# Gated cross-attention kernel: evictions, column-sum copy and GpSimd normalisation in another order, projection moved forward

## What is computed

```python
x = x + tanh(g_xattn[0]) * L0_xattn(layernorm(x), ctx, ctx, ...)   # pruned attention
x = x + tanh(g_ffn[0])   * L0_ffn(layernorm(x), ...)               # FP4 weights, gated
x = x + tanh(g_xattn[1]) * L1_xattn(ctx, layernorm(x), ...)        # linear attention
x = x + tanh(g_ffn[1])   * L1_ffn(layernorm(x), ...)               # int8 linear

# L0_xattn, one head
scores  = softmax(q @ k.T / 4)
col_sum = scores.sum(over queries)
keep the 460 keys of 512 with the largest col_sum, zero the others
out     = (scores * mask) @ v
```

## Time and profile before

| | us |
|---|---|
| median of 3 runs | 1252.24 |
| lowest and highest | 1250.3, 1255.97 |
| the profiled execution | 1255.39 |
| its span, first to last instruction | 1253.7 |

### The profile page before, as it was taken

One profiled execution on the slowest core, in us unless ns is written; L12 is line 12 of the kernel. 1 busy time (PEld: TensorE's weight loads), 2 busy tenths in 40 slices (PEclk: granted clock), 3 DMA queues, 4 the chain that ended last, 5 costly groups with the idle time before them and its releaser, 6 DMA issues.

```text
span 1253.7 us, 18028 instructions
## 1 busy us (share of the span) xinstructions
PE 1102.6 (88%) x5672; PEld 493.0 (39%) x5672; DVE 1004.8 (80%) x1977; ACT 944.4 (75%) x2135; POOL 236.0 (19%) x281
## 2 busy tenths in 40 slices
PE   7898898889898888889987879888999999999974
PEld 5433332222222222222321112224667677777652
DVE  7888877787787887787889886355899999999965
ACT  5566678889888898898979996465666776766744
POOL 5433320010011011101010101101222222222212
PEclk9999998999899999999989999989999999999986
DMA  9603141232123122213202211001011111110001
GB/s 289 167 34 88 58 110 31 48 93 55 50 68 71 52 58 66 60 30 94 46 25 51 44 50 41 18 5 42 27 51 43 35 59 43 35 60 26 18 17 34
DMA packets 75986, 71.79 MB, mean 57 GB/s; under 512 B 11834, under 2 KB 69492, under 8 KB 75892
## 3 DMA queue, kind: packets, MB, share of 16 engines
q1 hardware_dynamic: 75892, 70.64, 20.8%
HBM read 42.83 MB, written 27.28 MB: 56 GB/s over the span
## 4 chain that ended last, share of the span: by engine, by line
PE 58%; ACT 18%; DVE 14%; issue 7%; SPq 1%; POOL 1%; DMA 1%; DVEq 0%; ACTq 0%; POOLq 0%
PE ps_s L1289 12%; PE ps_a L1712 11%; ACT ea L1428 8%; PE ps_b L1670 6%; ACT prob L1444 6%; PE ps_b L1253 4%; DVE nmax L1329 3%; PE ps_s L1303 3%; PE ps_a L1253 3%; PE ps_s L1670 2%; PE ps_f L805 2%; PE ps_f L1685 2%; PE ps_f L834 2%; PE ps_a L1721 2%; PE ps_f L1746 1%
## 5 line engine op out<-in xcount | busy, mean ns | idle before, releaser
L1428 ACT ACTIVATE ea<-ps_a,nmax 128x512 f32<-128x512 f32 x512 | 356.2, 723 | 50.4 <-DVE nmax L1329 50.0
L1329 DVE TENSOR_REDUCE nmax<-ps_a 128x2 f32<-128x1024 f32 x256 | 312.5, 1221 | 98.9 <-PE ps_a L1253 97.4
L1289 PE MATMUL ps_s<-ea,rz 128*32 128x512 f32 x1024 | 283.1, 632 | 32.4 <-DVE rank L1372 30.1
L1303 PE MATMUL ps_s<-prob,v_pad 128*32 128x512 f32 x1024 | 282.3, 632 | 2.8 <-DVE att L1396 2.4
L1444 ACT ACTIVATE prob<-ps_b 128x1024 f32<-128x1024 f32 x214 | 228.3, 1067 | 21.8 <-PE ps_b L1253 21.2
L1712 PE MATMUL ps_a<-wgu,xT 128*128 128x352 f32 x512 | 166.2, 465 | 11.8 <-ACT ea L1887 9.2
L1253 PE MATMUL ps_b<-q_st,k_st 52*128 52x512 f16 x512 | 106.3, 395 | 42.4 <-ACT prob L1444 39.2
L1428 ACT ACTIVATION_READ_ACCUMULATOR ea<-ps_a,nmax 128x1 f32 x512 | 123.5, 241 | 0.0
L1253 PE MATMUL ps_a<-k_st,q_st 48*128 48x512 f16 x512 | 102.3, 395 | 20.5 <-ACT ea L1428 19.3
L1712 PEld LDWEIGHTS ps_a<-wgu,xT 128*128 128x128 f32 x512 | 92.8, 191 | 68.4 <-issue 24.3
L1887 ACT ACTIVATE ea<-ps_a 128x352 f32<-128x352 f32 x128 | 59.7, 467 | 58.0 <-PE ps_a L1712 57.5
(11 more groups left out here) (276 smaller groups left out, 1773.1 us busy)
## 6 DMA issues: line engine op xcount, KB each, us to landing
k_scr<-k_p SPq DMA_DIRECT2D x24, 256.0 KB, 2.5
q_scr<-q_p SPq DMA_DIRECT2D x24, 256.0 KB, 2.9
q_st<-q_scr SPq DMA_DIRECT2D x32, 192.0 KB, 4.7
k_st<-k_scr SPq DMA_DIRECT2D x32, 192.0 KB, 5.0
c_in<-in_ctx SPq DMA_DIRECT2D x8, 512.0 KB, 4.2
x_in<-in_x SPq DMA_DIRECT2D x8, 512.0 KB, 5.2
v_scr<-v_s SPq DMA_DIRECT2D x8, 512.0 KB, 4.2
v_in<-v_scr SPq DMA_DIRECT2D x16, 256.0 KB, 3.2
```

The source lines that it names most:

```text
L1289: e.matmul(ps_s[32 * h:32 * h + 32, :], rz[:, t, r, 2 * k + h, o:o + 32], ea[g % RING][:, 2 * k + h], start=(n == 0 and k == 0), stop=(n = ...
L1303: e.matmul(ps_s[o:o + 32, :], v_pad[u % 2][:, t, 4 * r + 2 * k + h], at.prob[g % PROBS][:, 2 * k + h], start=(t == 0 and k == 0), stop=(t ...
L1329: e.tensor_reduce(nmax[u % 2][:, t].rearrange("p (h r) -> p r h", h=2)[:, r], ps_a[:, z % 2 * 2:z % 2 * 2 + 2], AX_X, ALU.max, negate=True ...
L1428: e.activation(ea[c % RING][:, g % 4], ps_a[:, g % 4], ACT.Exp, bias=nmax[u % 2][:, t, n:n + 1], accum_out=tot[u % 2][:, t, n:n + 1]).then ...
```

## The change

It has six parts, made together.
- `BEFORE, RATE` go from 67, 0.7 to 100, 0.5: 100 pieces of projection lie in steps 0 to 40, the others from step 41 on at every second step, up to step 213 (before: 211).
- ACT's step is cut in two: first exponentials, then the evictions of `ended(z)`, then the second exponential (`later`). `leaving` is gone.
- `rank_step(u, 0)` moves ahead of the maxima of its step.
- `normal` for batches 2 to 7 moves from ACT to POOL, at the same fills and ahead of what POOL does there; PE's transposes wait for `s_pool_xn`.
- From step 256 on PE issues the second scores of z - 42 instead of z - 43 (both in step 256).
- The bias columns share the semaphore `s_turned`, with the counts moved on by one. This frees one semaphore.

```diff
@@ leave / done / bias_columns: s_bcol becomes s_turned
-            ins.then_inc(s_bcol, 1)
+            ins.then_inc(s_turned, 1)
-            e.wait_ge(s_turned, k + 1)
+            e.wait_ge(s_turned, k + 1 + (k >= TURNS.index(WQ)))
@@ project
-    BEFORE, RATE = 67, 0.7
+    BEFORE, RATE = 100, 0.5
@@ project, gpsimd
+        def normal(b, half):
+            p = b % 2
+            e.wait_ge(s_dve_nb, b + 1)
+            for t in (2 * half, 2 * half + 1):
+                ins = e.tensor_scalar(ey.x_in[p][:, t], ey.x_in[p][:, t], rs[p][:, t:t + 1], nb[p][:, t:t + 1],
+                                      ALU.mult, ALU.add)
+            if half:
+                ins.then_inc(s_pool_xn, 1)
 ...
+            if 0 < b < B - 1 and k in (GRAM, ROW):
+                normal(b + 1, int(k == ROW))
@@ project, tensor
-                e.wait_ge(s_act_xn, b + 1)
+                if b < 2:
+                    e.wait_ge(s_act_xn, b + 1)
+                else:
+                    e.wait_ge(s_pool_xn, b - 1)
@@ project, scalar
-                elif k in (GRAM, ROW):
-                    normal(b + 1, int(k == ROW))
@@ attend, tensor
-            b = within(z - LAG - 1, ALL_Z)
-            if b is not None:
-                second(b)
+            if z <= ALL_Z:
+                b = within(z - LAG - 1, ALL_Z)
+                if b is not None:
+                    second(b)
+            if z >= ALL_Z:
+                b = within(z - LAG, ALL_Z)
+                if b is not None:
+                    second(b)
@@ attend, vector
+            u, n = (z - HALVES - 4) // HALVES, (z - HALVES - 4) % HALVES
+            if 0 <= u < UNITS and n == 0:
+                rank_step(u, n)
             if z < ALL_Z:
                 maxima(z)
 ...
-            if 0 <= u < UNITS and n < 2 * ROUNDS + 2:
+            if 0 <= u < UNITS and 0 < n < 2 * ROUNDS + 2:
                 rank_step(u, n)
@@ attend, scalar: step ends after first(2 * z + 1)
+
+        def later(z):
             b = within(z - LAG, ALL_Z)
             if b is not None:
                 second(b)
@@ run, scalar
                 step(z)
-                for s in leaving(z):
+                for s in ended(z):
                     fill_and_magnitude(s)
+                later(z)
```

More of the change, by code:

```diff
@@ L214, in prepare @@
     s_gate, s_turned = m.sem("gate"), m.sem("w_turned")
-    s_w8q, s_w8t, s_bcol = m.sem("w8_rounded"), m.sem("w8_turned"), m.sem("bias_turned")
+    s_w8q, s_w8t = m.sem("w8_rounded"), m.sem("w8_turned")
     names = {WQ: "L0_xattn_Wq", WK: "L0_xattn_Wk", WV: "L0_xattn_Wv", WO: "L0_xattn_Wo", WK1: "L1_xattn_Wk",
@@ L336, in done @@
         def done():
-            e.wait_ge(s_turned, 6)
+            e.wait_ge(s_turned, 7)
             e.wait_ge(s_w8t, 1)
-            e.wait_ge(s_bcol, 1)
         return gate, leave, done
@@ L355, in bias_columns @@
         def bias_columns():
-            e.wait_ge(s_bcol, 1)
+            e.wait_ge(s_turned, 3)
             e.tensor_scalar(ey.cols[:, 0], bank[3][:, 0:DC], 0.25, None, ALU.mult)
@@ L611, in project @@
         m.sem(f"dve_{n}") for n in ("x1", "rb", "kv", "mean", "row", "c1w"))
-    s_act_m, s_act_gram, s_pool_r = m.sem("act_m"), m.sem("act_gram"), m.sem("pool_r")
+    s_act_m, s_act_gram, s_pool_r, s_pool_xn = (m.sem(n) for n in ("act_m", "act_gram", "pool_r", "pool_xn"))
     s_pe_xT, s_pe_cT, s_pe_q, s_pe_k, s_pe_v = (m.sem(f"pe_{n}") for n in ("xT", "cT", "q", "k", "v"))
@@ L1408, in step @@
                     reciprocals(g)
-            u, n = (z - HALVES - 4) // HALVES, (z - HALVES - 4) % HALVES
-            if 0 <= u < UNITS and n < 2 * ROUNDS + 2:
+            if 0 <= u < UNITS and 0 < n < 2 * ROUNDS + 2:
                 rank_step(u, n)
@@ L1456, in step @@
                 second(b)
-        return step
+        return step, later
     at.sync, at.gpsimd, at.tensor, at.vector, at.scalar = sync, gpsimd, tensor, vector, scalar
@@ L2255, in ended @@
             return pj.ends_at.get(z, ())
-        def leaving(z):
-            return [*(ended(z) if z <= pj.open else ()), *(ended(z + 1) if z >= pj.open else ())]
         @block.sync
@@ L2378, in _ @@
             gate()
-            step = at.scalar(e)
+            step, later = at.scalar(e)
             def fill_and_magnitude(s):
```

## The result

The changed kernel takes 1192.09 us (median of 4 runs, 1190.68 to 1192.89) against 1251.72 us for the kernel before beside it; the ratio is 0.9517, 95% interval 0.9492 to 0.9542. The direction was right, 60 us were gained where 39 were forecast.

A forecast was written before the change was run, and what follows sets the result against it. PE and DVE together were taken to bound the first stage, ACT the second and third. Terms +25 (first), -51 (second), -4 (third) and -9 (tail) gave -39 us: 1213 us for the median, range 1195 to 1242.

The forecast's parts named there:

- What bounds the stages: After the change: PE bounds the first stage at 94% busy, ACT the second at 95% or more.
- Rank copy: Copying sums ahead of maxima leaves 7 of ACT's 27.9 us of second-stage waits and takes 4.0 us off the third.
- No wait of PE over 0.5 us: Sign in the profile: no PE wait for the copy of the column sums longer than 0.5 us.
- Evictions: Second stage: ACT's 24.0 us of waits ahead of evictions should go to about 10, the mean's wait staying in part.
- Rival 1: Second exponentials, late by 0.69 us, starve PE; second stage ends at 450 us, the whole at 1232; chance 0.14.
- Tail: From step 256, second scores one step sooner: PE's waits beside gate_or_up go, -8, last exponential -1; bounds -4 and -12.
- Normalisation: 24 instructions leave ACT, 8.7 us of them in the second stage; on GpSimd they take 9.6 to 15.8 us.
- Rival 4: First stage: 16 GpSimd normalisations each stop DVE through the shared port, +6 to +11 us, total 1221; chance 0.06.
- First stage, +25: Steps 0 to 40: PE's 112.6 us plus 29.7 for 33 pieces plus 8 idle give 150.5; lower bound +21, upper +62.
- Rival 2: First stage: pieces set the pace through three PSUM banks, 1.88 us each, +62 us; total 1250, no change; chance 0.08.
- rival 3: First stage: crowded pieces wait for the previous step's evictions, 5.2 us a step, +87 us, total 1275; chance 0.07.
- Second stage, -51: Steps 41 to 211: ACT busy 411.6, idle 17, and 1.5 more for PE give 430 us; bounds -64 and -37.

The follow-up runs named there:

- e7: Kernel before with only the copy of the column sums moved ahead of the maxima: 1228.4 us, ratio 0.9792.
- e3: Changed kernel with the copy of the column sums back behind the maxima: 1219.9 us, ratio 0.9733 to the kernel before.
- e8: Kernel before with only ACT's step cut in two and evictions between first and second exponentials: 1238.7 us, ratio 0.9887.
- e2: Changed kernel with ACT's evictions back behind the second exponential and one step ahead: 1205.2 us, ratio 0.9622 to the kernel before.
- e6: Kernel before with only the schedule changed, BEFORE, RATE at 100, 0.5: 1243.1 us, ratio 0.9918.
- e5: Changed kernel with PE's second scores in the tail back at z - 43: 1201.8 us, ratio 0.9586 to the kernel before.
- e4: Changed kernel with the normalisation of batches 2 to 7 back on ACT: 1194.2 us, ratio 0.9534 to the kernel before.
- e1: Changed kernel with the schedule back, BEFORE, RATE at 67, 0.7: 1191.5 us, ratio 0.9512 to the kernel before.
- e11: Changed kernel with 33 more pieces ahead, BEFORE, RATE at 133, 0.32: 1211.2 us, ratio 0.9658 to the kernel before.
- e9: Changed kernel with RATE at 0.7 and BEFORE still 100: 1199.0 us, ratio 0.9561 to the kernel before.
- e12: Changed kernel with schedule back at 67, 0.7 and half the contraction of X1, GRAM, K, Q, V left out (output wrong): 1172.7 us, ratio 0.9349.

## Why the prediction was right and wrong, point by point

- **What bounds the stages: right.** PE the first (96%), ACT the second (97%), ACT the third (99%).
- **Rank copy: right.** Forecast were -21 in the second stage and -4 in the third; alone it brings -19.1 and -4.2 there (e7), undone +20.0 and +3.9 (e3). Of ACT's 27.9 us of waits 7 were to be left; it is 11.8, all of them for maxima (10.2 before), while the wait for the second scores went altogether. "No wait of PE over 0.5 us" was wrong: six in the second stage, of up to 1.1 us, are left, and one of 1.4 in the third.
- **Evictions: right in kind, and the size partly by luck.** Their waits were to go from 24.0 to 10 us, -14; they went to 0.3. e8 gives -16.7 in the stage, e2 +11.2. The forecast did not see that the moved pieces take much of the same waits away (e6), so that both parts claim them. Rival 1, that late second exponentials starve PE, is excluded by e8: alone the new order makes the kernel 15 us faster, and PE's waits for second exponentials are 18.6 us in the second stage, no longer than before (19.7). In company with the rest they do grow, from 25.7 (e2) to 34.8, while the 16.6 for first exponentials go.
- **Tail: right.** -9 forecast, -9.8 measured, or -10.9 by the last product of values; 8.6 of these by the mechanism named (e5), 2.3 by the rank copy, for which nothing was put in the tail.
- **Normalisation: a size.** 24 instructions at 0.40 to 0.66 us were bounded, the group in the first stage says 0.574:

```profile
L755 POOL TENSOR_SCALAR x_in<-x_in,rs,nb 128x256 f32<-128x256 f32 x16 | 8.9, 574 | 0.0
```

  Rival 4, the port, was worth 2 us at most (e4). By the Trainium skill's rule (SBUF — State Buffer, "SBUF: two separate sides") whoever comes second on the shared port waits for the whole instruction, and the rule is only for DVE operations in a 2-port mode, or with two SBUF inputs beside a GpSimd operation that reads SBUF; the earlier trace rows showed such a wait for c1w. What I had not weighed is how seldom it meets. Of DVE's 228 instructions in this stage 13 overlap one of the 16 normalisations, four of these are longer than their like elsewhere in the stage, by 0.7 us together, and four are maxima, which read PSUM and keep their 1.23 us.
- **First stage, +25: mis-sized, +15.9.** The sum was 112.6 + 29.7 + 8 = 150.3 (the text has 150.5); measured it is 110.0 (PE's old work, e1) + 25.5 + 6.2 idle = 141.7. The largest miss is the price of a piece on PE, 0.90 us, taken as a slope between the second and the third stage and carried to the first. Between e1 and the changed kernel PE's busy time grows there by 25.5 us for 33 pieces, 0.77 each, and in e6 by 23.8; in the second stage the same pieces take 32.0 us off it (405.2 to 373.2), 0.97 each. So the price came from a stage where a piece is dearer for PE; why it is, no run settles. The half clock does not inflate that slope: the third stage, which is subtracted, had as large a share of it (10.2 of 100.8 us, against 34.1 of 481.2), and with both taken to the full clock the slope is 0.93. The clock is a term of its own: fewer stretches at half of it were forecast, but the sum has nothing for them. From 13.7 to 3.4 us, with PE busy all through such a stretch, it is some 5 us of PE's time here (an estimate), which lies in the 110.0 and the 25.5. Rival 2, 1.88 us a piece, and rival 3, crowding, did not happen up to 100 pieces; at 133 the price rose to 1.02 us (e11).
- **Second stage, -51: mis-sized, -63.8.** The step that failed is the one that let the moved pieces count in the second stage with ACT's 9.0 us of evictions alone, on the ground that ACT was the bound. They bring 20.7 us in company (e1) and 31.4 alone (e6). The 9.0 themselves were near: by the starts of its instructions ACT's evictions differ by 8 us between e1 and the changed kernel. What was put at nothing is the pauses that the pieces cause ACT by keeping PE behind, some 13 us more by the same count; e9 and e12 show them, and e12 that they go when PE's work alone is thinned. With ACT busy 89% and PE 88%, neither was the bound alone. In the records this reads as 404.9 us busy where 411.6 were forecast and 12.5 idle instead of 18.5. PE's busy time, forecast at 392.5, was 373.2, and 17 of these 19 us are the half clock's (34.1 us of it before, none after), again a term that the sum lacks; what it is worth in a stage bound by ACT no run isolates.
- **What the parts bring alone and in company.** e6, e7 and e8 alone bring 10, 26 and 14 us (0.8, 2.1 and 1.1% of 1252), the tail 9 and the normalisation 2 (from e5 and e4, where they are undone): 61, and the whole is 60. Yet each part undone singly gives -1, 27, 13, 9 and 2, in sum 50: with all the others made, the schedule's 10 us are not there. The 33 pieces moved ahead add nothing to the final kernel.
- **Range.** Its lower end, 1195, was the sum of the favourable bounds (1193) pulled in, with the remark that they hardly meet. Second stage and first both came out at or beyond their favourable bound (-63.8 of -64, +15.9 where +21 was the bound). A higher clock is in both, but no run shows how much of either it makes.

## What to carry to other kernels

With two engines both busy near 90%, a piece of work moved away was worth more here than its share on the fuller one, and the worth of the move shrank when the stalls beside it were mended; measure such a move last. A wait that holds one engine for 2 us every 16 steps is cheap to find (one releaser, one count for each unit) and here was nearly half of the gain, by moving one instruction ahead of another. Check the price of moved work in the stage that it goes to: here a piece took PE 0.97 us in the one and 0.77 in the other. And where a forecast expects fewer stretches at half the clock, its sum needs a term for them.

## What the runs showed of the hardware

ACT's records lengthen while it runs without a pause, and the pace doesn't change. In the kernel before, the second exponential took 1.02 us at 659.82, growing step by step to 1.31 at 688.95, and 1.02 again at 692.32, behind a pause of 0.72 us:

```profile
688.95 1.31 ACT L1444 ACTIVATE prob<-ps_b 128x1024 f32<-128x1024 f32 x1
...
692.32 1.02 ACT L1444 ACTIVATE prob<-ps_b 128x1024 f32<-128x1024 f32 x1 [0.72 <-PE ps_b L1253]
```

All the while ACT's next instruction starts 0.90 us behind the start of this one, in both kernels (medians of 212: 0.905 before, 0.903 after). The group's mean rose from 1067 ns before to 1174 after, in a kernel that is 60 us faster, and single records reach 1.69 us. So a mean duration of back-to-back ACT instructions is no price, the starts of successive ones are; and ACT's busy time, made of such records, hides short pauses. And the halved clock comes and goes with PE's pauses: 58 us of it over three stages before, 31 with only the rank copy mended (e7: 10.2, 16.9 and 3.6), 34 with only that undone (e3), 3.4 in the changed kernel.
